# Graph convolution's layer norm: one GpSimd power in place of an integer guess and three Newton steps

## The reference

```python
s = _attention(xt, W1_s, W2_s, False)
h = jnp.einsum('bnm,bmct->bnct', s * A[None], xt)
g = jnp.einsum('bnct,cf->bnft', h, W_gcn)
y = _conv2d(jnp.swapaxes(g, 1, 2), tcn_w, tcn_b, STRIDE, 1) + x_res
y = jax.nn.relu(y)
z = jnp.transpose(y, (0, 3, 2, 1))
mu = z.mean(-1, keepdims=True)
var = ((z - mu) ** 2).mean(-1, keepdims=True)
z = (z - mu) / jnp.sqrt(var + 1e-05) * ln_g + ln_b
```

## Time and profile before

| | us |
|---|---|
| median of three runs | 1740.32 (1725.6 to 1743.68) |
| the profiled execution | 1733.57 |
| its span in the trace | 1731.7 |
| busy: TensorE, VectorE, ScalarE, GpSimd | 1425.5, 1051.8, 768.2, 609.1 |

### The profile page before, as it was taken

How to read it: one execution, slowest core, us unless ns; L and a number is a source line. 1 busy time by engine, 2 the same in 40 slices (tenths; PEclk the granted TensorE clock), 3 DMA queues, 4 the chain that set the end, 5 groups by cost and what they waited for, 6 DMA issues and landing times. The chain is left out here.

```text
span 1731.7 us, 27002 instructions
## 1 busy us (share of the span) xinstructions
PE 1425.5 (82%) x8422; PEld 1185.3 (68%) x8422; DVE 1051.8 (61%) x2259; ACT 768.2 (44%) x1222; POOL 609.1 (35%) x910
## 2 busy tenths in 40 slices
PE   6698999997582599999999956788999996377676
PEld 5596887886582488888888846687888885244443
DVE  5323788887348445444445326463788887488885
ACT  5322555554350233233333225223555554288885
POOL 1100456556212445566555321000455656100000
PEclk9799999999675699999999965798999999599999
DMA  7451121211581255565555278821121221112322
GB/s 237 123 157 38 47 73 64 78 58 64 192 265 57 69 115 112 131 140 99 112 124 109 31 161 288 261 83 37 47 82 55 81 68 60 55 56 84 100 88 64
DMA packets 97738, 180.13 MB, mean 104 GB/s; under 512 B 15184, under 2 KB 33152, under 8 KB 97668
## 3 DMA queue, kind: packets, MB, share of 16 engines
q1 hardware_dynamic: 75396, 135.16, 24.8%
q0 software_dynamic: 16384, 31.51, 10.6%
q10 hardware_dynamic: 5888, 12.59, 2.0%
HBM read 113.12 MB, written 66.10 MB: 103 GB/s over the span
## 5 line engine op out<-in xcount | busy, mean ns | idle before, releaser
L922 PE MATMUL g_y<-L_z,L_pt 128*128 128x192 f32 x1024 | 195.4, 334 | 1.5 <-ACT L_pt L1137 0.5
L922 PEld LDWEIGHTS g_y<-L_z,L_pt 128*128 128x128 f32 x1024 | 165.2, 192 | 6.8 <-ACT L_pt L1137 6.8
L1082 POOL TENSOR_TENSOR L_xr<-L_xr,L_lnb 128x192 f32<-128x192 f32 x128 | 105.5, 852 | 177.8 <-DMA L_xr<-x 92.0
L1455 POOL DMA_INDIRECT sums<-x_yo,x_places x64 | 102.9, 1609 | 141.9 <-ACT x_yo L1658 131.9
L1129 ACT ACTIVATE L_e<-g_s,L_nm 128x512 f32<-128x512 f32 x128 | 88.0, 687 | 78.8 <-DVE L_nm L970 77.5
L890 PE MATMUL g_z<-L_kw,L_xnT 96*128 96x192 f32 x512 | 91.8, 331 | 20.6 <-DVE L_v L1000 20.4
L1089 POOL TENSOR_TENSOR L_t<-L_rstd 128x48 f32<-128x48 f32 x96 | 28.9, 301 | 223.7 <-DVE L_rstd L1024 218.7
L1567 DVE TENSOR_TENSOR x_mid<-ex_g,x_sig 128x480 f32<-128x480 f32 (+1 forms) x48 | 31.4, 654 | 123.4 <-ACT x_sig L1649 123.4
L890 PEld LDWEIGHTS g_z<-L_kw,L_xnT 96*128 96x128 f32 x512 | 82.3, 189 | 29.9 <-DVE L_v L1000 29.9
L979 DVE SCALAR_TENSOR_TENSOR L_p<-L_e,L_rl,L_adj 128x512 f32<-128x512 f32 x128 | 99.1, 775 | 4.5
L970 DVE TENSOR_REDUCE L_nm<-g_s 128x1 f32<-128x512 f32 x128 | 87.5, 683 | 18.8 <-PE g_s L899 18.0
(11 more groups left out here) (345 smaller groups left out, 3890.6 us busy)
## 6 DMA issues: line engine op xcount, KB each, us to landing
L_xnT<-xn_rows SPq DMA_DIRECT2D x48, 384.0 KB, 3.3
x<-L_y SPq DMA_DIRECT2D x32, 384.0 KB, 2.6
xn_rows<-L_xnT SPq DMA_DIRECT2D x54, 192.0 KB, 3.9
L_xr<-in_x SPq DMA_DIRECT2D x24, 384.0 KB, 3.4
L_xr<-x SPq DMA_DIRECT2D x24, 384.0 KB, 3.4
L_raw<-xn_rows SPq DMA_DIRECT2D x16, 384.0 KB, 3.6
ff_xa<-x SPq DMA_DIRECT2D x16, 384.0 KB, 3.9
ff_xr<-x SPq DMA_DIRECT2D x16, 384.0 KB, 3.5
```

The costliest lines, as they stand in the source:

```text
L922: last = nc.tensor.matmul(out, pt[k % 2][:, P * c:P * c + P], z[q][:, c, :], start=False, stop=(c == NK - 1))
L1082: last = nc.gpsimd.tensor_tensor(v_, v_, gain(s.lnb), ALU.add)
L1455: nc.gpsimd.indirect_dma_start(sums, row(places[e % 2][:, 1, t:t + 1]), yo[t % 4][:, :], None, compute_op=ALU.add).then_inc(sent[t % 4], 16)
```

## The change

VectorE no longer forms a guess: after the reduction it scales the sum and adds epsilon, writes the result to `hvar` and hands over. GpSimd raises `hvar` to the power of a 128x48 tile that is filled with -0.5 and writes `rstd`, in one operation. Two waits are added: VectorE's, before it writes `hvar`, for the reciprocal root of the sample before, and GpSimd's, before it writes `rstd`, for the division of the sample before. The tiles `t1` and `guess` and the constant 1.5 go.

```diff
                     step(nc.vector.tensor_reduce(flat(s.var), oct_(sq), AX, ALU.add))
-                    step(nc.vector.tensor_scalar(s.var[:, :, :], s.var[:, :, :], 1.0 / O, 1e-5, ALU.mult, ALU.add))
-
-                    nc.vector.tensor_scalar(s.hvar[:, :, :], s.var[:, :, :], 0.5, None, ALU.mult)
-                    step(nc.vector.tensor_scalar(s.guess[:, :, :], s.var[:, :, :].bitcast(I32), 1, None,
-                                                 ALU.arith_shift_right))
-                    nc.vector.tensor_scalar(s.rstd[:, :, :].bitcast(I32), s.guess[:, :, :], -1.0,
-                                            float(0x5F3759DF), ALU.mult, ALU.add).then_inc(guess_done, 1)
+                    dve.wait_ge(rstd_done, free(b, 1))
+                    nc.vector.tensor_scalar(s.hvar[:, :, :], s.var[:, :, :], 1.0 / O, 1e-5, ALU.mult,
+                                            ALU.add).then_inc(guess_done, 1)
...
-                        chain.begin(b * 11)
                         pool.wait_ge(guess_done, ready(b))
-                        r, v1, w1 = s.rstd[:, :, :], s.hvar[:, :, :], s.t1[:, :, :]
-                        for n in range(3):
-                            chain(nc.gpsimd.tensor_tensor(w1, r, r, ALU.mult))
-                            chain(nc.gpsimd.tensor_tensor(w1, w1, v1, ALU.mult))
-                            chain(nc.gpsimd.tensor_tensor(w1, s.c15[:, :, :], w1, ALU.subtract))
-                            last = nc.gpsimd.tensor_tensor(r, r, w1, ALU.mult)
-                            if n < 2:
-                                chain(last)
-                        last.then_inc(rstd_done, 1)
+                        pool.wait_ge(scaled, ready(b - 1))
+                        nc.gpsimd.tensor_tensor(s.rstd[:, :, :], s.hvar[:, :, :], s.mhalves[:, :, :],
+                                                ALU.pow).then_inc(rstd_done, 1)
                         pool.wait_ge(scaled, ready(b))
```

More of the change, by code:

```diff
@@ L157, in fill @@
         self.nc.vector.memset(self.s.mhalf[:, :], -0.5)
-        self.nc.vector.memset(self.s.c15[:, :, :], 1.5)
+        self.nc.vector.memset(self.s.mhalves[:, :, :], -0.5)
         self.nc.vector.memset(self.s.ones[:, :], 1.0)
@@ L771, in _ @@
                             psm[z % 2][:, :, 0:2 * CT], ACT.Copy).then_inc(out_done, 1)
-CENTRE_STEPS, NORM_STEPS = 3, 6
+CENTRE_STEPS, NORM_STEPS = 3, 4
 def graph_conv(nc, s, tag, xn_rows, x_in, x_out, prefetch=None):
@@ L786, in graph_conv @@
          recip_done, sq_done,
-         guess_done, newton_done, rstd_done, scaled, out_done, base_done, gained) = s.sems(
+         guess_done, rstd_done, scaled, out_done, base_done, gained) = s.sems(
             tag,
@@ L791, in graph_conv @@
             "recip_done sq_done "
-            "guess_done newton_done rstd_done scaled out_done base_done gained")
+            "guess_done rstd_done scaled out_done base_done gained")
         xnT, xr, kron, kw = [s.xnT0, s.xnT1], [s.xr0, s.xr1], [s.k0, s.k1], [s.kw0, s.kw1]
@@ L1074, in _ @@
                 pool.sem_inc(rstd_done, LEAD)
-                chain = Chain(pool, newton_done)
                 with pool.Fori(0, B // 2) as i:
@@ L2343, in conv_buffers @@
     s.hvar = sb("hvar", [P, NK, T])
-    s.t1 = sb("t1", [P, NK, T])
     s.rstd = sb("rstd", [P, NK, T])
-    s.guess = sb("guess", [P, NK, T], I32)
     s.lng = sb("lng", [P, O])
@@ L2408, in build @@
         s.mhalf = sb(top, "mhalf", [P, 2])
-        s.c15 = sb(top, "c15", [P, NK, T])
+        s.mhalves = sb(top, "mhalves", [P, NK, T])
         s.ones = sb(top, "ones", [P, P])
```

## The result

The changed kernel takes 1797.91 us (median of 4 runs, 1791.49 to 1801.28) against 1735.24 us for the kernel before on the same chip: ratio 1.036, interval [1.029, 1.043]. The forecast had the sign right and three times the size: 1928 us, 188 above the median then shown, where about 63 came. The profiled execution of the changed kernel took 1791.49 us, 57.9 more than the profiled execution before (1733.6).

A forecast was written before the change was run, and what follows sets the result against it. TensorE was taken to bound the loop, the Newton chain hidden; a 12.2 us power adds 82.2 us in the loop and 14.8 at the ends, 97 per convolution: 1733.6 + 194 = 1928 us, range 1716 to 2000 (8 in 10).

The forecast's parts named there:

- the power's price: GpSimd's 128x48 power, its time called P: 0.50 us beyond a product at two columns taken per column, giving 12.2 us.
- With only 0.06 us of it fixed: Doubt on GpSimd's power: some start-up would take 1.4 us off its time and 46 off the sum.
- The bounds, 0.8 and 14.5: GpSimd's power in us: 0.80 if the extra is all start-up, 14.5 if even less of the small power is fixed.
- From P to the period: Convolution loop closing through VectorE's division: period is the power's time + 10.6, so 22.8 us, 5.87 more per sample.
- From P = 6.3 us on: Convolution loop: it feels the power only from this length, then each us costs 32 us, one per sample.
- the ends: Last two divisions of each convolution, where nothing hides GpSimd's work: about 7.4 us more each, 14.8 per convolution.
- The clock's term: TensorE's stall before the projections halves its clock: up to 26 x 1.9 = 49 us, giving 1977; set against possible start-up.
- VectorE's earlier hand-over: VectorE to GpSimd, after the reduction: 0.54 us earlier per sample, worth nothing by itself inside the loop.
- New waits: VectorE waiting for the previous reciprocal root, GpSimd for the previous sample: already passed when reached, cost nothing.
- The likeliest: Slow case, GpSimd's power above 6.8 us: own range 1851 to 2000 us; chance 0.66.
- The cheap power: Rival: GpSimd's power takes 0.8 to 3 us, only the convolutions' last divisions gain, 11 us, giving 1722; chance 0.18.
- the special treatment of -0.5: Rival: GpSimd's power with this exponent is a short root; falls together with the cheap power, no chance of its own.

The follow-up runs named there:

- 12.2 us at full clock: Changed kernel with a second, idle power of 24 columns ahead of the real one, plus 20 idle products on TensorE before the projections: ratio 1.116.
- 6.35: Changed kernel with the power on 36 of the 48 columns and a plain product on the other 12: ratio 1.007.
- 24 columns: Changed kernel with the power on 24 of the 48 columns and a plain product on the others, 4.4 us together: ratio 0.999.
- the three operations back: Changed kernel with VectorE's three removed operations put back on idle tiles ahead of the hand-over: ratio 1.057.
- the probe: Kernel before with idle GpSimd powers of 1 to 192 columns, other exponents and bases, ahead of the first convolution; its whole time means nothing.
- 8 or 20 idle products: TensorE products before the projections: 8 added to the changed kernel with VectorE's three operations back, 1.052; 20 added to that with a second 24-column power, 1.116.
- the later division: Changed kernel with VectorE's division moved one turn on, ahead of the split of u and v: ratio 1.010.

## Why the prediction was right in sign and wrong in size

- **The step that failed is the power's price**, "a price per column, it is 0.25 us a column, and P = 0.20 + 48 x 0.25 = 12.2 us". Measured are 0.159 us a column and 0.37 us fixed, P = 8.03. Of the 0.50 us at two columns 0.18 were a longer start and only 0.32 the columns. One row of two columns can't split the two, and I let the power start as cheaply as a product (0.20 us) because both are operations of GpSimd; no row said so. "With only 0.06 us of it fixed" was the right doubt with a third of the size. The bounds, 0.8 and 14.5, held the value. The 4.17 us too much, 32 times, are 133 of the 134 us between the forecast of 1928 and the sum with the right P below.
- The Trainium skill's page "GPSIMD Engine Reference", section "Performance versus the Vector engine", whose 2.6 cycles an element agreed with the trace for products, would have given an estimated 0.3 us for the power. The measured 8.03 us decides: that rule doesn't carry over to it.
- **From P to the period: shown.** "The period is P + 10.6": (418.73 - 268.67)/8 = 18.76 us after, which is 8.03 + 10.7; with 12.2 us at full clock 22.9, which is 12.2 + 10.7. "From P = 6.3 us on": no loss at 4.4, 0.1 us a sample at 6.35.
- **The sum holds with the right P.** 14 x (8.03 + 10.6 - 16.93) = 23.8; the ends 8.13 - 4.33 - 0.54 = 3.3 and 8.13 - 4.33 - 0.82 = 3.0; together 30 us a convolution. Measured: 32.1 and 30.4. Added to the profiled execution before, 1733.6 + 60 = 1794, against 1791.5. That the whole times agree to 3 us is in part luck: the two convolutions grew by 62.5 us, and the stretch between them, which no edit touches, happened to be 5.2 us shorter. Two slips in the recorded sum are too small to matter: the rows give 0.69 us where 0.6 is taken off the path, and the two ends add up to 14.6, not 14.8.
- **The clock's term was right for P = 12.2,** and letting it "cancel" against a part of the start-up was poor bookkeeping: one is a matter of P, the other of a gap at a given P, and each had a trace to be argued from. At 8.03 us the gap is 0.8 to 1.6 us and the term nearly nothing: in 23 of 26 turns the projections take 1.95 us, in three, each behind a gap of 1.5 us, 2.13 to 2.29.
- **VectorE's earlier hand-over "is worth nothing by itself" inside the loop:** right as long as TensorE is the bound (24 columns: no gain). In the changed kernel the hand-over lies in the ring and its 0.54 us count in full: with the three operations back the period is 19.3. The prediction's 1.17 us from reduction to hand-over had them left out already.
- **New waits cost nothing:** right. The power starts 0.08 us behind the scaling, and the division's row names the power alone.
- **The cases.** The likeliest came true, P above 6.8, but only 1.2 us beyond its edge and so below its own range, which began at 1851 us; the wide range held the time. The cheap power fell with the probe, and with it the special treatment of -0.5.

## What to carry to other kernels

One small instance of an operation gives one equation for two unknowns, its start and its price per column: keep both ends open and take a value between them, or measure two sizes. What replaces a chain counts by its latency, not by its number of instructions: here one of 8.03 us took the place of twelve that needed 5.23 with their hand-overs, and the loop's slack of about a microsecond decided how much of that showed. Work out that slack first, for beyond it each microsecond is paid once per turn, and a gap that it opens on TensorE can cost again through the clock.

## What I had not expected of the hardware

- GpSimd's power costs the same for 16 and for 128 partitions, and for any base and exponent tried: 0.159 us a column, where a product of 48 to 192 columns pays 2.1 ns.
- In the run with VectorE's part back, the clock fell in 17 of 21 turns with a gap of 2.0 to 2.15 us before the projections; in the changed kernel, with gaps of 0.8 to 1.6 us, in three of 26. With 8 or 20 idle products in the gap it was granted in full.
- VectorE's centring and residual, which have two large inputs, take about a third longer beside GpSimd's additions and products: in the changed kernel the centring averages 1.23 us and the residual 0.97, with the later division the centring 0.96 and the residual 1.32, whichever of them lies beside GpSimd's work. Row probabilities, which have two as well, take from 0.76 to over 1 us beside the additions and 0.75 alone. The one long power costs them nothing: the centring of 0.96 us lies beside it in the kernel with the later division, as do row probabilities of 0.75 us in the changed kernel.
